# Mamba rounds: skip rows and state inputs from one product, and eight of sixteen states scaled by ScalarE

## The reference, cut to what matters

```python
xv = silu(conv(x @ W_in) + conv_b)              # 256 channels
ssm = xv @ W_x                                   # 40 columns: dt_raw 8, Bp 16, Cp 16
delta = softplus(dt_raw @ W_dt + b_dt)
dA  = exp(delta[..., None] * A)                  # 16 states
dBx = delta[..., None] * Bp[:, :, None, :] * xv[..., None]
h   = associative_scan(dA, dBx)                  # along the 512 tokens
y   = einsum('bldn,bln->bld', h, Cp) + xv * D
s   = y @ W_out
x   = x + s * silu(ffn(xn))
```

## Time and profile before

| | value |
|---|---|
| median of 3 runs | 754.86 us (753.48 to 755.99) |
| the profiled execution | 754.58 us, span 752.7 us |
| busy over the span | PE 665.7, DVE 645.0, ACT 501.6, POOL 490.3 us |
| scans, 128 of 128x1024 | 288.5 us on DVE |
| POOL's drives products, 127 | 304.6 us |
| states added by DVE (284 instructions) | 77.9 us |
| states scaled by ACT (188 instructions) | 52.8 us |

### The profile page before, as it was taken

The page is one execution under the profiler, slowest core; times in us unless marked ns, Lnnn a source line. Parts: engine busy times, 40 slices in busy tenths (PEclk is TensorE's granted clock), DMA queues, the critical chain, the costliest instruction groups (busy, mean ns, idle before and its releaser), DMA issues. The chain is left out here.

```text
span 752.7 us, 12948 instructions
## 1 busy us (share of the span) xinstructions
PE 665.7 (88%) x4001; PEld 491.8 (65%) x4001; DVE 645.0 (86%) x1102; ACT 501.6 (67%) x1020; POOL 490.3 (65%) x305
## 2 busy tenths in 40 slices
PE   1898999999799998768998998998999999988785
PEld 0885555655565553446876787787777777768765
DVE  5878877777567656989999999999999999999997
ACT  1565666666444444879879778788788797796463
POOL 1001663000055445086999999999999999999995
PEclk9999999999999999989999999999999999999999
DMA  7900110001222217534424336237046156254000
GB/s 203 294 1 7 39 40 28 0 0 28 60 64 68 71 48 98 169 147 127 108 99 128 98 113 144 69 113 182 30 150 151 38 158 154 76 130 120 1 15 16
DMA packets 43050, 67.43 MB, mean 90 GB/s; under 512 B 6264, under 2 KB 30208, under 8 KB 42992
## 3 DMA queue, kind: packets, MB, share of 16 engines
q1 hardware_dynamic: 31744, 48.35, 20.4%
q0 software_dynamic: 9520, 17.78, 11.6%
q10 hardware_dynamic: 1728, 0.57, 0.3%
HBM read 46.01 MB, written 9.67 MB: 74 GB/s over the span
## 5 line engine op out<-in xcount | busy, mean ns | idle before, releaser
L1710 DVE TENSOR_TENSOR_SCAN xnT_all<-psum,nfT_all 128x1024 f32<-128x1024 f32 x128 | 288.5, 2275 | 0.1
L1260 PEld LDWEIGHTS psum<-W_out,xnT_all 128*128 128x128 f32 x2048 | 237.3, 193 | 56.9 <-issue 54.2
L1260 PE MATMUL psum<-W_out,xnT_all 128*128 128x128 f32 x2048 | 242.7, 277 | 29.5 <-DVE acc L1726 27.3
L1433 ACT ACTIVATE psum<-delta,A 128x511 f32<-128x511 f32 x256 | 165.0, 683 | 59.8 <-DVE xnT_all L1710 59.7
L1240 POOL TENSOR_TENSOR nfT_all<-nf_rows,du 128x1024 f32<-128x1024 f32 x63 | 147.2, 2361 | 23.0 <-DVE nfT_all L1792 22.5
L1240 POOL TENSOR_TENSOR nfT_all<-attn_all,du 128x1024 f32<-128x1024 f32 x64 | 157.4, 2601 | 1.1 <-DVE xnT_all L1710 1.1
L571 POOL DMA_INDIRECT moe_dram<-xnT_all x39 | 37.6, 963 | 119.9 <-ACT xnT_all L827 119.9
L1726 DVE SCALAR_TENSOR_TENSOR acc<-psum,Cc,acc 128x128 f32<-128x128 f32 x284 | 77.9, 338 | 6.1 <-PE psum L1260 6.1
L560 POOL DMA_INDIRECT xs_dram<-nf_rows,pos x32 | 33.1, 1036 | 76.3 <-DVE pos L881 57.3
L1260 PE MATMUL psum<-vo_all,W_taps 128*128 128x512 f32 (+3 forms) x128 | 58.7, 606 | 0.7 <-ACT vo_all L1465 0.7
L1484 ACT ACTIVATE ts<-psum,Cc 128x128 f32<-128x128 f32 x188 | 52.8, 360 | 4.1 <-PE psum L1260 4.1
(11 more groups left out here) (218 smaller groups left out, 1128.0 us busy)
## 6 DMA issues: line engine op xcount, KB each, us to landing
nf_rows<-bt_dram SPq DMA_DIRECT2D x32, 512.0 KB, 4.7
attn_all<-bt_dram SPq DMA_DIRECT2D x32, 512.0 KB, 3.9
delta<-rl POOLq DMA_DIRECT2D x7, 512.0 KB, 7.0
e<-ab POOLq DMA_DIRECT2D x7, 512.0 KB, 5.8
delta<-e POOLq DMA_DIRECT2D x7, 512.0 KB, 6.1
xs_dram<-attn_all SPq DMA_DIRECT2D x4, 645.0 KB, 8.3
xnT_all<-xs_dram SPq DMA_DIRECT2D x39, 64.5 KB, 1.9
x_all<-in_x_dram SPq DMA_DIRECT2D x8, 256.0 KB, 6.0
```

The lines of the kernel that those rows point to most:

```text
L1260: return nc.tensor.matmul(o, l, r, start=start, stop=stop)
L1433: ins = nc.scalar.activation(dA[:, i % RA, k, 1:L], delta[:, p, h, 1:L], ACT.Exp, scale=A[:, h, 2 * q + k:2 * q + k + 1])
L1710: nc.vector.tensor_tensor_scan(hring[:, i % R, :, :].rearrange("p n l -> p (n l)"), dA[:, i % RA, :, :].rearrange("p n l -> p (n l)"), dbx ...
```

## The change

1. `skip` and `ssm` become one product `rows`: xv is stationary, and W_rows (W_outD and W_x side by side, 168 columns) moves, in 16 passes, into both banks of bM. ACT copies the 40 columns of state inputs (`in_rows`) and the 128 skip columns out (`rows_out`, at q = 0), PE turns the 40 columns back by four transposes (`turn_rows`, between the projections of states 0 and 1), and ACT copies those into ssmT (`ssm_out`, now at q = 1). `C_rows` goes; Cp is read from `in_rows`.
2. ACT takes states 8 and 14 as well. `scale_state` of state n stands at quarter n // 2 + 1, behind that quarter's `decays`; 14 and 15 stand in the next round's q = 0, behind `decays` of pair 1.
3. The eight scaled states lie in `early` (four) and `late` (four). POOL adds early onto late by one transfer of 1 MB (`fold`, q = 3 of the next round), and three additions follow (two at q = 5, one at q = 6) in place of five.
4. The softplus transfers of L1191 and L1196 become one of 1 MB at q = 6, behind both ACT results; `delta<-e` stays at q = 7 and waits for it.
5. The output of sequence b - 1 is summed at q = 7 of round b, gated and completed at q = 0 and 1 of round b + 1, and stored by SP at q = 2.

```diff
-        ON_ACT = (5, 7, 9, 11, 12, 15)
+        ON_ACT = (5, 7, 8, 9, 11, 12, 14, 15)
+        FOLD = len(ON_ACT) // 2
...
+                    def fold():
+                        pool.wait_ge(S["ts"], at(b - 1, "ts", len(ON_ACT)))
+                        alone(pool)
+                        pool.dma_start(late[:, :, :, :], early[:, :, :, :], accum_op=ALU.add).then_inc(s_sp, 16)
+                    def sum_folded(i):
+                        if i == 1:
+                            pool.wait_ge(s_sp, summed(b, 1))
+                            alone(pool)
+                            pool.wait_ge(S["os"], at(b - 2, "os", 1))
...
+                    def softplus_sums():
                         w("lg", 1)
                         w("rl", KH)
                         w("e1", 1)
                         alone(pool)
+                        pool.dma_start(delta_e1[:, 1 - p:3:1 + p, :, :], rl_ab[:, :, :, :], accum_op=ALU.add)\
+                            .then_inc(s_sp, 16)
                     def deltas():
-                        pool.wait_ge(s_sp, b * 48 + 32)
+                        pool.wait_ge(s_sp, summed(b, 1 + end))
...
                         for q in range(NP):
-                            if q in (1, 2, 3) and end:
-                                sum_scaled(b - 1, q + 1)
-                            if q == 4 and end:
-                                sum_scaled(b - 1, 5)
-                                output_sum()
+                            if q == 0 and b > 1:
+                                output_gate(b - 2)
+                            if q == 1 and b > 1:
+                                output_rows(b - 2)
+                            if q == 3 and end:
+                                fold()
+                            if q == 5 and end:
+                                sum_folded(1)
+                                sum_folded(2)
...
+                    def rows():
+                        w("xv", KH)
+                        for j in range(TPB):
+                            for h in range(KH):
+                                ins = mm(both[:, j // 2, j % 2, :], xv[:, h, j * P:(j + 1) * P], W_rows[:, h, :],
+                                         h == 0, h == KH - 1)
+                        ins.then_inc(S["acc_ps"], 1)
+                    def turn_rows():
+                        w("C", 1)
+                        w("acc0", 1)
+                        for j in range(TPB):
+                            ins = nc.tensor.transpose(bank[bM[0]][0:RX, j * P:(j + 1) * P], in_rows[:, 1 - p, j, :], ident)
+                        ins.then_inc(S["ssm_ps"], 1)
...
                         if q:
                             project(2 * q - 2)
+                            if q == 1 and prep:
+                                turn_rows()
                             project(2 * q - 1)
...
+                    def rows_out():
+                        w("acc_ps", 1)
+                        drained(act, b - 1, NS - 1)
+                        drained(act, b - 1, NS - 2)
+                        nc.scalar.activation(in_rows[:, 1 - p, :, :].rearrange("p (b j) e -> p b j e", b=2),
+                                             both[:, :, :, D:D + RX], ACT.Copy).then_inc(S["C"], 1)
+                        act.wait_ge(S["acc"], at(b - 1, "acc", TPB))
+                        nc.scalar.activation(skip_sb[:, 1 - p, :, :].rearrange("p (b j) d -> p b j d", b=2),
+                                             both[:, :, :, 0:D], ACT.Copy).then_inc(S["acc0"], 1)
...
                         if scan and q + 1 < NP:
                             decays(b, p, q + 1)
-                        if q == 0 and end and scan:
-                            scale_state(b - 1, 1 - p, 5)
-                        if scan and 3 <= q < 8:
-                            scale_state(b, p, q - 3)
+                        if scan:
+                            for n in (2 * q - 2, 2 * q - 1):
+                                if n in ON_ACT:
+                                    scale_state(b, p, n)
+                                elif n < 0 and n + NS in ON_ACT and end:
+                                    scale_state(b - 1, 1 - p, n + NS)
```

More of the change, by code:

```diff
@@ L479, in attention_moe_mamba_ffn @@
         RA = 2
-        ON_ACT = (5, 7, 9, 11, 12, 15)
+        ON_ACT = (5, 7, 8, 9, 11, 12, 14, 15)
+        FOLD = len(ON_ACT) // 2
+        LAST = sum(n < NS - 2 for n in ON_ACT)
         ON_DVE = tuple(n for n in range(NS) if n not in ON_ACT)
@@ L1120, in round_, with store @@
                             .then_inc(s_bst, 16)
[L1121 to L1122 removed]
+                    def store(c):
+                        sp.wait_ge(S["ow"], at(c, "ow", 1))
                         alone(sp)
[L1124 removed]
+                        sp.dma_start(out[ds(c, 1)].rearrange("a (j p) d -> p (a j) d", p=P), ow[:, :, :])\
                             .then_inc(s_o, 16)
@@ L1136, in round_ @@
                                 .then_inc(s_bld[q], 16)
[L1137 to L1140, removed]
+                            if b > 1 and q == 2:
+                                store(b - 2)
+                    elif scan:
+                        store(b - 2)
+                        store(b - 1)
+                    else:
+                        store(b - 1)
                 rounds(sp, round_)
@@ L1214, in round_ @@
                         for q in range(NP):
[L1215 to L1220 removed]
+                            if q == 0 and b > 1:
[7 more added lines that the diff above has]
+                                sum_folded(2)
+                            if q == 6:
                                 if prep:
[L1222 removed]
+                                    softplus_sums()
                                 if end:
[L1224 to L1226 removed]
+                                    for i in range(3, FOLD):
+                                        sum_folded(i)
                             if q == 7:
[L1228 to L1229 removed]
                                 if prep:
                                     deltas()
[L1232 removed]
+                                if end:
+                                    output_sum()
                             pool.wait_ge(s_bld[q], (b + 1) * 16)
@@ L1244, in round_ @@
                             drives()
+                        else:
+                            output_gate(b - 1)
+                            output_rows(b - 1)
                     elif end:
-                        for i in range(2, len(ON_ACT) - 1):
-                            sum_scaled(b - 1, i)
-                        pool.wait_ge(S["accP"], at(b - 1, "accP", len(ON_ACT) - 1))
+                        for i in range(1, LAST):
+                            sum_last(i)
+                        pool.wait_ge(S["accP"], at(b - 1, "accP", LAST - 1))
                         pool.wait_ge(S["G1"], at(b - 1, "G1", 1))
@@ L1363, in round_ @@
                             if q == 0:
-                                ssm()
-                                skip()
+                                rows()
                             elif q == 1:
-                                C_rows()
                                 dt(0)
```

91 lines of the change are left out of this document (48 added, 43 removed).

## The result

The changed kernel takes 763.38 us (median of 6 runs, 761.3 to 766.83), the one before 755.79 (6 runs beside it, 753.48 to 757.59): a ratio of 1.0104, 95% interval [1.0072, 1.0137]. It is slower by 1%. The profiled execution took 765.6 us with a span of 763.8, which is 11.1 over the span before.

What follows compares the result with a forecast made beforehand. A round was taken as a DVE stretch then a PE stretch, bound by two hand-overs. On the profiled 754.58 us, 8.7 + 2.1 - 0.7 - 0.9 = +9.2 gave 763.8 us, range 755.5 to 769.5.

Steps and rivals of the forecast that it cites:

- State 8 to ACT: ACT drains state 8 behind pair 6's decays, so PE projects state 10 later after pair 5's scans: +1.29 us a round.
- S: End of pair 5's scans on DVE, at 575.80 in the profile before; starts the stretch to PE's projection of state 10.
- States 14 and 15: From their projection to DVE adding state 1, ACT's copies and new rows net +0.16 us a round (11.32 against 11.16).
- Y: Start of PE's projection of states 14 and 15, at 591.12 in the profile before; state 1 followed 11.16 us later.
- Six intervals: The six full rounds with `x_in`, each longer by 1.29 and 0.16 us: +8.7 us together.
- The merged transfer, M = 9: M is the landing time of the 1 MB softplus transfer POOL issues, taken as 9 us; bounds 5.8 and 14.0.
- Round 6 to 7: Interval into the last round, without `x_in`: the 1 MB transfer delays pair 1's scans, +2.1 us; landing in 5.8, -1.0.
- Head -0.7, tail -0.9: Head: DVE's wait for state 0 in round 0 shortens, -0.7 us; tail: only scans follow state 8 in round 7, -0.9.
- Cover that was named: Work expected to be hidden: POOL's fewer additions win nothing, `fold` lands in time, additions in the tail cost nothing (uncovered +1).
- Rival 1: DVE's list decides everywhere, so two states of 1.02 us leave seven intervals, one the tail: -15.3, 739.3 us; chance 0.12.
- Rival 2: ACT drains state 8 in time for PE, so the 1.29 us a round fall away: +1.5, 756.1 us; chance 0.08.
- Rival 3: The 1 MB softplus transfer delays every round, from a landing time of 11.0 us; at 14.0, 787 us; chance 0.08.

Runs made afterwards that it cites:

- The first experiment: Changed kernel with ACT copying state 8 between the two halves of pair 6's decays instead of behind both: 756.98 us, 1.0012 of the kernel before.
- the second experiment: Changed kernel with ACT copying states 14 and 15 between the halves of pair 1's decays instead of behind both: 756.53 us, 1.0009 of the kernel before.
- the third experiment: Changed kernel with states 8, 14 and 15 all copied early, between the halves of those decays, merged transfer kept: 754.38 us, 0.9979 of the kernel before.

## Why the prediction was right, point by point

The forecast was 763.8, slower; the median is 763.38.

- **State 8 to ACT, +1.29 a round: right.** S is 582.65 in this round and PE starts state 10 at 585.27, 2.62 later against 1.30 before: +1.32. The first experiment shows the cause.
- **States 14 and 15, +0.16: right in size.** Y is 599.34 and state 1 starts at 610.72, 11.38 against 11.16: +0.22. The 168 columns take 2.28 us (2.4 taken) and the input copy 0.30 (0.3 taken). But the hand-over itself costs 1.29, as the second experiment shows; the term was small because PE and DVE give back 1.1 at the same place.
- **Six intervals, +8.7:** measured +9.49, a round of 54.66 where 54.53 was forecast. The other signs that were named are there too: DVE's busy time falls from 51.19 to 49.42 us a round and its idle time grows by 3.3, state 1 waits 1.14 for PE, and POOL waits 1.34 at `delta<-e`.
- **The merged transfer, M = 9: over-sized.** It measures 7.6. The Trainium skill (DMA: Bandwidth & Descriptors, Anatomy of one DMA) gives an estimate of 4.4 for 1 MB; the trace disagrees by 3 us. The lower of the two bounds from rows, 5.8, and the value taken, 9, enclose what was measured.
- **Round 6 to 7, +2.1: near in size (+1.70), wrong in make-up.** (The two times that it was taken from, 701.8 and 699.8, give 2.0.) The way through POOL held: with M = 7.6 the first scan of round 7 is due M + 18.4 = 26.0 us after the end of pair 3's scans, and it starts 26.00 after it (704.54 - 678.54), with ACT's decays ready only then too; pair 1's come 5.84 later, where 5.9 was forecast. So this part is +0.62, as M = 7.6 makes it. The step that failed is "at M = 5.8 only state 8's -1.0 is left": it took round 7 to have no second hand-over, since it has no `x_in`. But states 14 and 15 stand there too, behind decays that wait for DVE, and that adds 1.08; moving these copies shortened that stretch by 1.26. With two transfers of 5.1 us the interval is still 1.47 us longer than before, and not 1.0 shorter. An over-sized transfer stood in for a hand-over that was not counted: that the sum came out near is luck in this term.
- **Head -0.7, tail -0.9:** measured -0.88 and -0.60. The 1.39 ahead of the first scan belong to neither; they may be a part of the 2.2 us by which the profiled execution exceeds the median.
- **Cover that was named:** POOL won nothing by its 14.5 us less work, `fold` with 7.5 us is met in time, and the additions in the tail cost nothing.
- **Rival 1, DVE is the bound (739.3): fell.** DVE's work fell and the round grew; 1.56 us more on DVE's list, where DVE waits for PE, leave the round as it is. The Trainium skill (Perfetto Trace Analysis, Identifying the Most-Contended Engine) would have the engine with the highest occupancy relieved; DVE's share fell from 86% to 83% and the time rose by 1%. The rule is half right all the same: once the copies stood where nobody waits for them, the same relief came with a gain, 0.2%, and 1.1% with the softplus transfer in two again. How much of that is the relief, and how much the product of 168 columns, no run separates.
- **Rival 2, ACT's drain costs PE nothing (756.1): fell** for the kernel as it is. The first experiment builds its condition, and comes to 756.98.
- **Rival 3, the merged transfer binds every round (787): fell**, by the two transfers' 54.67. It binds a round of the third experiment, once the hand-overs are gone.

Still open: why the merged transfer took 10.0 us in one round of the third experiment and 7.7 to 8.4 in the others. B loads were in flight beside it in that round (issued at 563.30 and 570.15), but in others too, as at 457.98 beside the transfer of 458.60; no run takes the load away alone.

## What to carry to other kernels

Before work is moved off the busiest engine, ask where the receiving engine's list will reach it, and who waits there: here four copies of 0.28 us, standing behind decays that wait for DVE, cost 1.3 to 1.4 us of every round in each of two places, and moving them ahead of half a pair of decays turned a loss of 1.0% into a gain of 0.2%, and of 1.1% with the transfer split as well. Price each hand-over of a round, the last round's too, and not only the work that goes. A merged transfer that costs 0.2 us today can be the next bound when the round gets shorter.

## What the runs showed of the hardware that was not expected

Three additions on DVE with both operands in SBUF (128x256, 4 bytes) took 6.43 us beside POOL's work; at the end of the same program, with POOL idle, an addition of twice the size takes 0.69. Memsets of 128x512 at the same place took 0.52 each (1.56 for three), and DVE's own scans and additions, which have one operand in PSUM, kept their durations (2.28 and 0.34 us on average, as in the changed kernel). In the tail of that run the two timelines stand side by side, DVE's three additions and POOL's last two:

```profile
781.78 4.12 DVE L1917 TENSOR_TENSOR spare_dve<-const 128x256 f32<-128x256 f32 x3
```

```profile
782.88 1.33 POOL L1286 TENSOR_TENSOR accP<-accP,G 128x512 f32<-128x512 f32 x1
784.30 1.33 POOL L1288 TENSOR_TENSOR accP<-accP,x_all 128x512 f32<-128x512 f32 x1
```

Here they take 1.37 each, the pace of POOL's additions (784.30 - 782.88 = 1.42). In the round shown above they start at 609.46, 611.91 and 614.40, the first two 2.45 and 2.49 long beside POOL's products, which start 2.31 and 2.51 apart, the third 1.41 beside the output's addition of 1.41: such an addition seems to last as long as the POOL instruction beside it. The pace is shown; that the two engines take turns at something is argued from it.

An adding transfer of 1 MB took 7.6 us where two of 512 KB took 5.1 each, so twice the size was not twice the time; but in one round of the third experiment it took 10.0, and that round was 3.5 us longer, a part of it at half the granted clock.
